# One PreLN attention and look-up feed-forward kernel: bank waits on the exponential, Wv's transposes moved behind the first mix, look-up steps placed anew

## The reference

```python
n = layernorm(x)
q, k, v = n @ Wq, n @ Wk, n @ Wv
scores = einsum('bes,bfs->bef', qT, kT) / sqrt(16)     # 512 x 512 for each batch
x = x + swap(softmax(scores) @ vT) @ Wo
n = layernorm(x)
gate, up = n @ lut[gate_idx].T, n @ lut[up_idx].T      # 1376 rows, each index picks one of 16 values
x = x + (silu(gate) * up) @ lut[down_idx].T
```

## Time and profile before

| what | us |
|---|---|
| median of 3 runs | 1014.46 |
| lowest and highest run | 1014.06, 1014.69 |
| the profiled execution, device time | 1014.02 |
| its span, first to last instruction | 1012.2 |
| PE busy | 980.4 (97%) |
| DVE busy | 547.3 (54%) |
| ACT busy | 450.8 (45%) |
| POOL busy | 140.8 (14%) |
| mean granted PE clock | 0.996 |

### The profile page before, as it was taken

The page is one execution under the profiler, slowest core; times in us unless marked ns, Lnnn a source line. Parts: engine busy times, 40 slices in busy tenths (PEclk is TensorE's granted clock), DMA queues, the critical chain, the costliest instruction groups (busy, mean ns, idle before and its releaser), DMA issues.

```text
span 1012.2 us, 12392 instructions
## 1 busy us (share of the span) xinstructions
PE 980.4 (97%) x4452; PEld 808.3 (80%) x4452; DVE 547.3 (54%) x1105; ACT 450.8 (45%) x720; POOL 140.8 (14%) x143
## 2 busy tenths in 40 slices
PE   5899979999999999999999999999999999999998
PEld 5898868787887768888888887888888888888886
DVE  6899899899999943332443244324432443243011
ACT  5899898888998821121222122212221222122111
POOL 2322300000000000111211121112111211121111
PEclk9999999999999999999999999999999999999999
DMA  7979902301111182220442034203420342031001
GB/s 242 231 178 155 176 6 91 131 8 48 52 51 71 57 322 86 103 63 21 84 166 63 21 84 167 63 21 84 166 63 21 84 166 63 22 84 42 1 1 41
DMA packets 98747, 91.06 MB, mean 90 GB/s; under 512 B 65072, under 2 KB 85440, under 8 KB 93632
## 3 DMA queue, kind: packets, MB, share of 16 engines
q1 hardware_dynamic: 84784, 76.63, 24.9%
q0 software_dynamic: 8864, 6.43, 4.9%
q10 hardware_dynamic: 5040, 7.21, 2.2%
HBM read 48.24 MB, written 35.59 MB: 83 GB/s over the span
## 4 chain that ended last, share of the span: by engine, by line
PE 79%; DVE 13%; ACT 3%; issue 3%; POOL 1%; DMA 1%; SPq 0%; ACTq 0%; DVEq 0%
PE bank L1086 41%; PE bank L1094 21%; PE bank L1028 12%; PE bank L1110 4%; DVE part L1245 3%; DVE picked L1245 2%; DVE bn L1222 1%; ACT part L821 1%; POOL rstd L777 1%; DVE w_lo L1264 1%; DVE xg_lo L1264 1%; DMA xg<-in_L_attn_x 1%; DVE smax L1418 1%; DVE part L1289 1%; DVE bit_mask L1252 0%
## 5 line engine op out<-in xcount | busy, mean ns | idle before, releaser
L1086 PE MATMUL bank<-x2t_hi,w_hi 128*128 128x512 f32 (+1 forms) x704 | 275.6, 391 | 6.8 <-DVE x2t_lo L1342 3.3
L1086 PE MATMUL bank<-x2t_hi,w_lo 128*128 128x512 f32 (+1 forms) x704 | 274.8, 390 | 0.0
L1086 PE MATMUL bank<-x2t_lo,w_hi 128*128 128x512 f32 (+1 forms) x704 | 274.7, 390 | 0.0
L1500 DVE TENSOR_TENSOR h_whole<-bank,h_silu 128x512 f32<-128x512 f32 (+1 forms) x66 | 45.6, 691 | 323.3 <-PE bank L1086 323.3
L1086 PEld LDWEIGHTS bank<-x2t_hi,w_hi 128*128 128x128 f32 (+1 forms) x704 | 130.7, 186 | 37.7 <-issue 5.1
L821 ACT ACTIVATE part<-high_bit,lut,lut_step 128x512 f32<-128x512 uint8 x198 | 152.9, 810 | 14.1 <-DVE part L1245 8.3
L1086 PEld LDWEIGHTS bank<-x2t_lo,w_hi 128*128 128x128 f32 (+1 forms) x704 | 130.9, 186 | 29.7
L1086 PEld LDWEIGHTS bank<-x2t_hi,w_lo 128*128 128x128 f32 (+1 forms) x704 | 130.8, 186 | 29.2
L772 POOL TENSOR_TENSOR h_lo<-h_whole,h_hi 128x512 fp32r<-128x512 f32 x60 | 84.7, 1412 | 481.1 <-ACT h_hi L1002 481.1
L1000 ACT ACTIVATE h_silu<-bank 128x512 f32<-128x512 f32 (+1 forms) x66 | 39.3, 596 | 228.6 <-PE bank L1086 228.6
L1094 PE MATMUL bank<-w_hi,h_hi 128*128 128x512 f32 (+1 forms) x324 | 126.7, 391 | 0.0
(11 more groups left out here) (156 smaller groups left out, 1319.8 us busy)
## 6 DMA issues: line engine op xcount, KB each, us to landing
x_planes_scratch<-x_planes SPq DMA_DIRECT2D x40, 256.0 KB, 2.2
xg<-in_L_attn_x ACTq DMA_DIRECT2D x5, 1024.0 KB, 5.8
m_hi<-m_scratch SPq DMA_DIRECT2D x5, 1024.0 KB, 7.3
m_lo<-m_scratch SPq DMA_DIRECT2D x5, 1024.0 KB, 9.3
x1a<-in_L_attn_x SPq DMA_DIRECT2D x4, 1024.0 KB, 4.8
out_dram<-x1a SPq DMA_DIRECT2D x4, 1024.0 KB, 3.9
x1b<-in_L_attn_x SPq DMA_DIRECT2D x3, 1024.0 KB, 5.2
out_dram<-x1b SPq DMA_DIRECT2D x3, 1024.0 KB, 3.9
```

Source lines behind the costliest of these rows:

```text
L1086: last = pe.matmul(tile[0:n, :], a, x, start=(k == 0 and j == 0), stop=(k == K - 1 and j == 2))
L1500: dve.tensor_tensor(h_whole[c % 2][0:n, :], bank[5][0:n, :], h_silu[c % 2][0:n, :], ALU.mult).then_inc(h_done, 1)
```

## The change

Three edits. In `groups` the first mix and turn_v trade places: the first mix is now items 24 to 27 (banks 0 to 3), turn_v 28 to 31 (banks 4 to 7). With it go the entries `ln1`, which hang on the first mix. The wait of the first transposes of block 0 keeps its number, 32, though it is written in another way. PE's wait for a bank that a score had last is now on `sexp_done`, the exponential, in place of the score's low half. And the look-up steps stand at other entries.

```diff
         groups = [(GRAM, 0), (GRAM, 1), (PROD, 0), (PROD, 1), (SCORE, 0), (SCORE, 1),
-                  (TURN_V, 0), (MIX, 0), (FOLD, 0), (MIX, 1), (FOLD, 1)]
+                  (MIX, 0), (TURN_V, 0), (FOLD, 0), (MIX, 1), (FOLD, 1)]
...
         ACT_LOOKS = (
...
-            "0000000000300000000000030000000000000000000060000000000000000400004010002000030000400002000030000400"
-            "0010000000000000300000002000000040000002000000500000020002000000000000000000000000000000000060003000"
-            "0300400300004003000020050000100300010000500100001010500000000204000040000070020400003000000600030003"
-            "04000000000300000405000605002060000400060400305001050006040020500104000606001050000e0005040020400001"
+            "0000000000300000000000020000000000000000000060000000000000000300003020002000030000400003000030000400"
+            "00100000000000002000000020000000300000020000004000000300020000000000000000000000000000000000a0003000"
+            "0500200300004003000040030000100500010000400100001020400000000205000020000080020600002000000800020002"
+            "0500000000020000060400060400305001050006040020500104000606001050000600060500106000060004040020500102"
         )
         DVE_LOOKS = (
...
-            "000000000006000000040000000400000005000000200000050000005010000000000000000000000000001000100a000300"
-            "0040060030000540200003300000052010003320020000600100007000000060202002007000009030000000902000802000"
-            "601000000000400000a04000d020060500402000d020080300702000c020060500502000d050040400i02000c02006040040"
+            "000000000005000000030000000400000006000000400000040000005010000000000100001000100100000000000a000400"
+            "007002005000062010000540100002301000440001000090011000600000007020000100a000008050000000705000601000"
+            "702000000000200000c02000d020080300702000c020060500502000d050040400602000d030070400404000a04006020090"
...
                 if b.first and t == 0:
-                    pe.wait_ge(product_lo, K * (number[(MIX, 0)] + 1))
+                    pe.wait_ge(product_lo, K * number[(FOLD, 0)])
...
-                    pe.wait_ge(product_lo, n - (2 if n // K < number[(MIX, 1)] else 1) * K + 1)
+                    bank_user = n - (2 if n // K < number[(MIX, 1)] else 1) * K
+                    if is_score(bank_user):
+                        pe.wait_ge(sexp_done, bank_user - K * number[(SCORE, 0)] + 1)
+                    else:
+                        pe.wait_ge(product_lo, bank_user + 1)
```

More of the change, by code:

```diff
@@ L462, in preln_attention_ghost_ffn @@
             "0000000000000000000000000000000000000000000000000000000000000000000000000000000000000000000000000000"
-            "0000000000000000000000000000000000001000007000010000000000000000000000000000000000300000000000000000"
-            "0000000000300000000000030000000000000000000060000000000000000400004010002000030000400002000030000400"
-            "0010000000000000300000002000000040000002000000500000020002000000000000000000000000000000000060003000"
-            "0300400300004003000020050000100300010000500100001010500000000204000040000070020400003000000600030003"
-            "04000000000300000405000605002060000400060400305001050006040020500104000606001050000e0005040020400001"
+            "0000000000000000000000000000000000001000007000020000000000000000000000000000000000300000000000000000"
+            "0000000000300000000000020000000000000000000060000000000000000300003020002000030000400003000030000400"
+            "00100000000000002000000020000000300000020000004000000300020000000000000000000000000000000000a0003000"
+            "0500200300004003000040030000100500010000400100001020400000000205000020000080020600002000000800020002"
+            "0500000000020000060400060400305001050006040020500104000606001050000600060500106000060004040020500102"
         )
@@ L470, in preln_attention_ghost_ffn @@
             "0000000000000000000000000000000000000000000000000000000000000000000000000000000000000000000000000000"
-            "0000000000000000000000020000000000000000009000000010000000000000000000000000002000000000001000000000"
-            "0000000100000000050000030000000030000000000008000000000000000050000300000700004000050000400004000020"
-            "000000000006000000040000000400000005000000200000050000005010000000000000000000000000001000100a000300"
-            "0040060030000540200003300000052010003320020000600100007000000060202002007000009030000000902000802000"
-            "601000000000400000a04000d020060500402000d020080300702000c020060500502000d050040400i02000c02006040040"
+            "000000000000000000000002000000000000000000a000000020000000000000000001000000001000000000000000000000"
+            "0000000100000000050000030000000020000000000008000000000000000050000300000700004000060000400004000010"
+            "000000000005000000030000000400000006000000400000040000005010000000000100001000100100000000000a000400"
+            "007002005000062010000540100002301000440001000090011000600000007020000100a000008050000000705000601000"
+            "702000000000200000c02000d020080300702000c020060500502000d050040400602000d030070400404000a04006020090"
             "1"
```

## The result

| | before | after |
|---|---|---|
| median of 20 runs each, us | 1014.57 | 1016.16 |
| lowest and highest | 1014.06, 1016.28 | 1015.47, 1019.63 |
| the profiled execution | 1014.02 | 1015.85 |
| its span | 1012.2 | 1014.0 |

The ratio is 1.0018, with a 95% interval of 1.0012 to 1.0024: the changed kernel is slower by 1.2 to 2.4 us. The ratio itself is within 0.2%, the upper end of its interval is not. The direction of the forecast (1013.1) was wrong, and the median lies just outside the range. What follows explains the 1.83 us between the two profiled executions (the medians are 1.59 apart).

A forecast was written before the change was run, and what follows sets the result against it. PE's work plus its gaps were taken to bound the kernel, with gaps up to 355 us read from DVE, which makes the weights. Terms -0.4 +1.7 -4.67 +2.0 gave -1.35 on 1014.46: 1013.1 us, range 1010.7 to 1016.0.

The forecast's parts named there:

- Step 1: First mix and turn_v: PE runs without a stop until 138.8 us and gains 3.3 us there.
- Step 2: First fold: ACT and DVE bind its start, 144.6 instead of 144.99; 0.4 us arrives, one gap of 5.8 remains.
- Step 3: First fold item: the clock falls to 1.2 GHz behind the 5.8 us gap, costing 1.7 us.
- first rival: At the fold: the clock is kept and the 1.7 us not paid, 1011.4 (about 1009.6 without G10's gap); 22%.
- G9's price: Up half of G9: 12 matmuls took 4.44 us instead of 2.72, so a fallen clock costs 1.7.
- Step 4: Up to G0: DVE must find 2.7 us for extra look-up steps; G0 at 195.5, same gap of 1.7.
- Step 5: G9 and G10: G9's 4.67 us stop goes, a 2.0 gap appears ahead of up G10, at 350.9.
- second rival: Ahead of G10: the new order idles DVE, making the look-up late; 1015.6 with 0.8 us, 1016.8 with 2; 22%.
- Sum: Up G10 at 350.9 instead of 352.24, -1.35 us, everything after it moving as one: 1013.1.

The follow-up runs named there:

- early_digits: Changed kernel with the look-up steps of the first 244 entries placed as before: 1016.01 us, ratio 1.0013.
- g10_first: Changed kernel with five DVE look-up steps moved from behind to ahead of the low half of H9: 1015.19 us, ratio 0.9999.
- digits_only: Kernel before with only the change's new look-up step placements, order and waits as before: 1016.69 us, ratio 1.0003.
- placed_filler: The kernel placed plus 20 matmuls without a use in PE's gap ahead of the first fold: 1013.25 us, ratio 0.9985.
- placed3_split: placed_filler with before's step counts from entry 394 to 439, missing steps handed back in parts by entries 460 and 461: 1014.74 us, ratio 0.9995.
- placed: Changed kernel with the edits of early_digits and g10_first, and one ACT look-up step moved from entry 491 to 495: 1014.01 us, ratio 0.9995.
- before_g9: Kernel before with six DVE look-up steps moved from behind to ahead of the low half of H7: 1015.90 us, ratio 1.0008.
- after_no_wait: Changed kernel with the old bank wait (product_lo) in place of the exponential: 1016.94 us, ratio 1.0020.
- placed3_late: placed_filler with before's step counts from entry 394 to 439, missing steps handed back behind G0: 1015.70 us, ratio 1.0011.
- old_digits: Changed kernel with before's look-up step strings, order and waits new: 1018.16 us, ratio 1.0032.
- before_filler: Kernel before with 8 matmuls without a use in the gap ahead of its fold: 1014.65 us, ratio 0.9996.
- filler: Changed kernel with 20 matmuls without a use in the gap ahead of the first fold: 1016.58 us, ratio 1.0011.
- after_region: Changed kernel with before's step counts from entry 394 to 439, handed back by entry 452 on ACT and 462 on DVE: 1022.10 us, ratio 1.0068.

## Why the prediction was wrong, step by step

- **Step 1** (the mix without gaps) came out as written: turn_v ends at 139.84. That is one microsecond later than the 138.8 worked out, and this microsecond is the first thing that went wrong. It doesn't come from the mix: the first matmul of the scores already starts at 105.28 in place of 104.26.

```profile
104.26 0.39 PE L1028 MATMUL bank<-mat_y_hi,wb_hi 128*128 128x512 f32 x1
```

```profile
105.28 0.39 PE L1028 MATMUL bank<-mat_y_hi,wb_hi 128*128 128x512 f32 x1
```

- **Step 2** is the first term that failed: the fold starts at 146.04, not 144.6. I had score 23 end at 137.4 on DVE. In after's DVE timeline, which answers to the earlier trace rows, it ends at 138.91, 0.11 later than before (138.13 + 0.67 = 138.80):

```profile
138.24 0.75 DVE L1432 SCALAR_TENSOR_TENSOR mat_x_lo<-full,srec,mat_x_hi 128x512 fp32r<-128x512 f32 x1
138.91 0.68 DVE L1414 TENSOR_TENSOR mat_y_lo<-bank,mat_y_hi 128x512 fp32r<-128x512 f32 x1
...
143.43 2.47 DVE L1414 TENSOR_TENSOR wb_lo<-bank,wb_hi 128x512 fp32r<-128x512 f32 x4
```

  Two terms make up these 1.5 us. The scores start 1.02 us later, which the prediction put at nothing. Of that, 0.42 are the look-up steps that the new digits place ahead of the scores: from PE's first matmul behind its gap at 51 us to the scores it is 54.07 us in after and 53.65 before, and early_digits, with before's digits there, has 53.63. The other 0.6 stand already in that matmul (51.21 against 50.61), which came anywhere from 50.75 to 51.58 in the six profiles of the new order with before's digits up to there, so they are not shown to be the change's doing. The second term is a size: counted from the first matmul of the scores, score 23's low half comes 0.91 us sooner than before (32.96 against 33.87), and DVE's waits between 126 and 139 us went from 2.18 to 1.07. So DVE did get idle time back, as I had said, but 0.91 us and not 1.4; the wait of 0.50 for ACT ahead of 136.56 is as long as before. What stands behind score 23, eight subtractions, three merges and a mask, took 6.99 us where I had 7.1.
- **Step 3** (the clock falls, as the first rival denied) was right, and mis-sized: 2.3 us in place of 1.7. I took G9's price. There the first eight matmuls took 0.42 us or more from start to start, here the first eleven (0.227 at full rate), so the clock stayed down for longer. Other executions with the same gap show 1.6 (g10_first: 7.17 from the fold to the transposes, less 5.57), so the size varies. The Trainium skill, "TensorE: Matmul & The Clock Gate", section "HAM oscillation — how this bites in real kernels", has the array fall to half rate in waits between bursts, and the trace agrees (0.50 behind 6.21 us). By the Trainium skill's section "A second HAM failure mode: psum-queue depth-cycling", same page, the old mix would have had half rate too; the rows of before and of digits_only's fold, 1.00 behind gaps of 2.01 and 2.77, do not bear that out, while a gap of 2.63 in digits_only's mix was followed by 0.60.
- **Step 4**: G0 at 197.60 and not 195.5. The 2.1 us are the 1.44 of step 2 and the 0.6 of step 3; its gap of 1.7 was right. I had asked whether DVE could find the 2.7 us of extra steps. It could only since PE was late: placed_filler and placed3_split show that with PE on time they cost 1.6 us.
- **Step 5**: G9's stop goes, as written, and up G10 has a gap of 1.84 where I had 2.0. Between them stands one that I had not seen, 0.97 us ahead of G4. In ACT's timeline a leaf waits 2.81 us for a merge on DVE, the four normalisations stand behind it, and the silu (h_gate) behind them:

```profile
237.70 0.82 ACT L821 ACTIVATE part<-high_bit,lut,lut_step 128x512 f32<-128x512 uint8 x1 [2.81 <-DVE part L1249]
238.42 2.92 ACT L877 ACTIVATE xn_second<-x_second,shift,rstd 128x512 f32<-128x512 f32 x4
241.24 0.58 ACT L971 ACTIVATE h_gate<-bank 128x512 f32<-128x512 f32 x1
```

  placed moves that one leaf and the gap shrinks to 0.27. This is the mechanism of my second rival (DVE and ACT idle by the new order), at another place than the one that I had named, and without a fall of the clock.
- **Sum.** Up G10 was put at 350.9 and came at 353.94: 1.44 (step 2) + 0.6 (step 3) + 0.97 (G4) is 3.01 of the 3.04. In terms of before the parts are +3.43 at G0, +0.97 at G4, -4.67 at G9, +1.84 at G10, together +1.57 of the 1.70 seen. One figure of the rivals is off by itself: 1014.46 - 3.05 - 2.0 is 1009.4 and not 1009.6, which changes no bound.

So the mechanisms of the sum (a gathered gap, a fallen clock, the stop moved from G9 to G10) were right, and the sign of the whole hung on terms of half a microsecond to one and a half. Two of them, the later start of the scores and G4's gap, were not in the sum at all, and two were off in size by about half a microsecond each, the time that DVE gets back (1.4 for 0.9) and the clock's price (1.7 for 2.3). What stays open is where the 0.6 us ahead of the scores come from, and why the same gap at the fold costs 1.6 us of clock in one execution and 2.3 in another.

## What to carry to other kernels

Ahead of a change that closes gaps on the busiest engine, find what the last of the gaps waits for: if another engine's chain sets that time, the gaps are only gathered into one, and one long gap can cost the clock where several short ones did not. When a change moves work of other engines, ask first whether the stretch that you reckon from still starts at the same time: here it began 1.02 us later, and that took away all that was gained inside it. Idle time inside a chain of answers (DVE to ACT to DVE) is spare in part only; here 0.9 of 1.4 us came back. When one engine's work is moved earlier to mend a late stop, count at each place that it passes what becomes late if the busiest engine is on time, since a fallen clock or an earlier gap may be hiding it.

## What the runs showed of the hardware beyond that

**A gap near 2 us and the clock.** Behind gaps of 1.84 (after), 2.01 (before), 2.15 (before_g9, at G9), 2.32 (placed3_split) and 2.77 us (digits_only) the clock stayed at 1.00; behind 1.86 (after_no_wait), 2.02 and 2.08 (before_g9), 2.63 (digits_only), 2.71 (placed3_late) and 2.79 us (before) it fell; behind the gaps of 4.2 us and more looked at here it fell every time. The price at the fold was 1.6 to 2.4 us behind 6.2 us and 2.8 behind 8.33 (old_digits). So one profile can't say what a gap of 2 to 3 us costs.

**A small fetch that lands late.** The index fetch of 64 KB lands after 1.8 us in the median of its 30 in a profile. In some executions the two issued at 87 and 94 us land far later. In placed's profile the tile's view of 84 to 112 us gives both, issue to landing, and behind it stands DVE's row:

```profile
DMA to landing us min/median/max: 15.7/18.8/21.8
```

```profile
109.24 0.23 DVE L1264 TENSOR_SCALAR high_bit<-idx_in 128x256 int16<-128x256 int16 x1 [12.76 <-DMA idx_in<-idx_scratch]
```

DVE's wait there was none in the profile of before, 1.45 us in before_filler's, 2.33 in after's, 2.44 in after_no_wait's, 4.28 in placed3_late's, 5.99 in digits_only's, 8.03 in filler's and 12.76 in placed's, and those executions took 1014.02, 1014.57, 1015.85, 1017.10, 1017.16, 1018.59, 1020.42 and 1023.17 us. The order is the same in both lists, but these are different kernels, and profiles without such a wait took up to 1021.10 us (after_region). For the long waits the trace shows the price: the fold starts at 151.26 in filler and at 155.45 in placed, against 146.04. The wait of 2.33 in after cost nothing: from the scores' first matmul to score 23's low half it is 32.96 us, and 32.97 in g10_first, which has the same digits there and no such wait. Such profiles are of little use up to the fold. Why the fetch lands late in some executions was not tried.
